# One core, four layers of attention and experts: learned-key attention by whole chunks, and divisions, stores and roots joined to their neighbours

## The reference, cut to what matters

```
def _layernorm(x, axis=-1, eps=1e-05):
    m = jnp.mean(x, axis=axis, keepdims=True)
    v = jnp.var(x, axis=axis, keepdims=True)
    return (x - m) / jnp.sqrt(v + eps)

def pattention(x, K, V):                 # K, V: learned, 128 keys (512 for the last one)
    a = softmax(scale * einsum('btc,nc->btn', x, K), axis=-1)
    return einsum('btn,nc->btc', a, V)

# layer 0 attention: softmax attention over q, k, v, then
# out = a_dot * (1 - w) + a_mem * w, where a_mem = (sigma_q @ memory) / (sigma_q @ memory_norm)

# layer 1 attention
        h = layer_norm(x)
        k = pattention(h, kK, kV)
        q = pattention(h, qK, qV)
        v = pattention(h, vK, vV)
        ...
        o = causal_sdpa(to_heads(q), to_heads(k), to_heads(v))
        o = o.transpose(0, 2, 1, 3).reshape(B, T, C)
        o = pattention(o, pK, pV)
        x = o + x_in
        x_inter = x
        x = pattention(layer_norm(x), fK, fV)
        return x + x_inter
```

## Time and profile before

| | us |
|---|---|
| median of 3 runs | 3603.91 (3601.78 to 3606.88) |
| profiled execution | 3613.86 |
| its span | 3612.1 |
| granted PE clock, mean over the span | 0.926 of full |
| busy: PE, DVE, ACT, POOL | 3240.8, 2450.0, 1820.7, 1191.2 |

### The profile page before, as it was taken

How to read it: one execution, slowest core, us unless ns; L and a number is a source line. 1 busy time by engine, 2 the same in 40 slices (tenths; PEclk the granted TensorE clock), 3 DMA queues, 4 the chain that set the end, 5 groups by cost and what they waited for, 6 DMA issues and landing times. The chain is left out here.

```text
span 3612.1 us, 39566 instructions
## 1 busy us (share of the span) xinstructions
PE 3240.8 (90%) x12845; PEld 1536.3 (43%) x12845; DVE 2450.0 (68%) x4164; ACT 1820.7 (50%) x2881; POOL 1191.2 (33%) x1010
## 2 busy tenths in 40 slices
PE   8899998999997699979998789898898789889999
PEld 5422224444444354535544233333333354764443
DVE  4788874443338577746544899999999955656544
ACT  5366672444446355534333777777777633312221
POOL 4211110000002222210000799999999910210000
PEclk7699998999998799989899899999999979889999
DMA  4222201000002533110000443443443410000000
GB/s 129 66 69 65 61 31 33 1 0 1 1 19 81 132 88 91 60 39 1 1 1 25 153 153 147 148 157 144 155 152 147 147 45 3 1 1 1 0 1 24
DMA packets 113335, 232.14 MB, mean 64 GB/s; under 512 B 27701, under 2 KB 82378, under 8 KB 95754
## 3 DMA queue, kind: packets, MB, share of 16 engines
q1 hardware_dynamic: 109034, 228.02, 19.0%
q0 software_dynamic: 4096, 1.59, 0.2%
HBM read 191.46 MB, written 34.87 MB: 63 GB/s over the span
## 5 line engine op out<-in xcount | busy, mean ns | idle before, releaser
L1199 DVE TENSOR_REDUCE a_top<-a_sc 128x1 f32<-128x512 f32 (+3 forms) x1024 | 547.2, 584 | 162.3 <-PE a_sc L1075 102.5
L2406 POOL TENSOR_TENSOR a_g<-a_g,a_spread 128x1024 f32<-128x1024 f32 x255 | 597.7, 2363 | 41.4 <-DVE a_g L2336 40.8
L2336 DVE TENSOR_TENSOR_SCAN a_g<-a_decay,a_drive 128x512 f32<-128x512 f32 x510 | 587.1, 1201 | 16.3 <-ACT a_drive L2225 12.9
L1156 ACT ACTIVATE a_prob<-a_st 128x1024 f32<-128x1024 f32 (+2 forms) x512 | 422.5, 862 | 280.7 <-PE a_st L1092 182.9
L705 DVE TENSOR_TENSOR f_s<-f_a,f_spread 128x512 f32<-128x512 f32 x392 | 269.4, 687 | 381.8 <-PE f_y L547 170.6
L2084 PE MATMUL a_y<-a_g,ident 128*128 128x512 f32 x1024 | 481.0, 610 | 31.3 <-POOL a_g L2406 31.3
L538 PE MATMUL f_hid<-h,f_w 128*128 128x512 f32 x784 | 404.2, 597 | 0.0
L547 PE MATMUL f_y<-f_s,f_w 128*128 128x512 f32 x784 | 401.6, 594 | 2.6 <-DVE f_s L705 2.6
L2209 ACT ACTIVATE a_decay<-a_delta,a_capped_a 128x512 f32<-128x512 f32 x512 | 331.8, 710 | 12.4 <-DVE a_g L2336 9.7
L1072 PE MATMUL a_sc<-a_k,a_q 96*128 96x512 bf16 (+3 forms) x1024 | 311.4, 357 | 20.9 <-POOL a_mask_k L996 11.2
L2084 PEld LDWEIGHTS a_y<-a_g,ident 128*128 128x128 f32 x1024 | 198.4, 197 | 306.7 <-issue 246.1
(11 more groups left out here) (396 smaller groups left out, 4903.0 us busy)
## 6 DMA issues: line engine op xcount, KB each, us to landing
a_spread<-a_bc_rows SPq DMA_DIRECT2D x128, 1024.0 KB, 4.6
a_q<-a_q_rows SPq DMA_DIRECT2D x192, 96.0 KB
a_pv_rows<-a_pv_sb SPq DMA_DIRECT2D x48, 256.0 KB, 2.0
a_k<-a_k_rows SPq DMA_DIRECT2D x288, 32.0 KB
a_k<-a_k_rows SPq DMA_DIRECT2D x288, 16.0 KB
a_num<-a_pv_rows SPq DMA_DIRECT2D x16, 256.0 KB, 3.6
a_pv_rows<-a1q_vf SPq DMA_DIRECT2D x16, 256.0 KB, 2.1
a_q_rows<-p_qp SPq DMA_DIRECT2D x24, 128.0 KB
```

Of the source, the lines that this page charges most:

```text
L1156: nc.scalar.activation(prob[w % 2][:, j, 0:width(kp)], st[:, j % 2, 0:width(kp)], ACT.Exp, scale=a.scale).then_inc(s.exp_done, 1)
L1199: nc.vector.tensor_reduce(top[:, t, n:n + 1], sc[:, slot(4 * n + t) % 3, 0:w], AX.X, ALU.max).then_inc(s.maxed, 1)
L2336: nc.vector.tensor_tensor_scan(to, decay[:, n % 4, k, way], drive[:, k, way], 0.0, ALU.mult, ALU.add).then_inc(scanned, 1)
L2406: nc.gpsimd.tensor_tensor(g[:, n % 8, :, :], g[:, n % 8, :, :], spread[:, pair % 4, 2 + n % 2:3 + n % 2, :].to_broadcast([P, H2, L]), ALU. ...
```

## The change

It has seven parts.

1. **Roots**: the Newton step is one reciprocal and three instructions that each do two operations.
2. **Output**: f3 stores each chunk of the output itself, after its last addition.
3. **Division**: `combine` uses buffers that `attend` has left free (`a.q`, `a.k`). Near the end of `attend`, SP loads the denominators of the first seven chunks and the numerators of chunks 0 to 3, POOL builds the selection matrices, and DVE takes the reciprocal. The denominators of the last chunk are loaded in `combine`, spread over 64 rows, and inverted as a 128x128 tile. The wait for the last store moves from `attend` into SP's list in `combine`.
4. **Learned keys**: a1p has a function of its own, `pattention_one`, which goes by chunks.
5. **layer0_project**: `copy_num` and `widen` stand ahead of the three squares.
6. **a1q**: the parts of k are stored ahead of those of q.
7. **Mamba**: one small Silu is put into its layer norm's block.

```diff
@@ layer_norm (the same in layer_norm_twice and mixture)
-            nc.vector.tensor_scalar(v[:, :], var[:, :], EPS, None, ALU.add)
             chain(nc.vector.reciprocal(rstd[:, :], std[:, :]))
-            chain(nc.vector.tensor_tensor(v[:, :], v[:, :], rstd[:, :], ALU.mult))
-            chain(nc.vector.tensor_tensor(v[:, :], v[:, :], rstd[:, :], ALU.mult))
-            chain(nc.vector.tensor_scalar(v[:, :], v[:, :], -0.5, 1.5, ALU.mult, ALU.add))
-            chain(nc.vector.tensor_tensor(rstd[:, :], rstd[:, :], v[:, :], ALU.mult))
+            chain(nc.vector.scalar_tensor_tensor(v[:, :], var[:, :], EPS, rstd[:, :], ALU.add, ALU.mult))
+            chain(nc.vector.scalar_tensor_tensor(v[:, :], v[:, :], -0.5, rstd[:, :], ALU.mult, ALU.mult))
+            chain(nc.vector.scalar_tensor_tensor(rstd[:, :], v[:, :], 1.5, rstd[:, :], ALU.add, ALU.mult))
@@ mixture, sync engine
+            if out is not None:
+                for c in range(NB):
+                    sp.wait_ge(f.added, c + 1)
+                    sp.dma_start(out[:, chunk(c)], S.x[:, chunk(c)]).then_inc(S.stored, 16)
+                sp.wait_ge(S.stored, 16 * NB)
@@ attend, sync engine
             for b in range(1, NB):
                 body(b, True, True, b % 2)
+            sp.wait_ge(s.st_done, (nB + NB - 1) * 32)
+            for k in range(2):
+                sp.wait_ge(s.pv_stored[k], 16 * 2 * (nB + NB - 1))
+            sp.dma_start(m.den[0:EARLY, :], m.rows[0:EARLY, DH, :]).then_inc(m.den_loaded, 16)
+            for b in range(4):
+                sp.dma_start(m.num[:, b, :], m.rows[H * b:H * b + H, 0:DH, :]).then_inc(m.num_loaded[b], 16)
             body(NB, False, True, 0)
-            for k in range(2):
-                sp.wait_ge(s.pv_stored[k], 16 * 2 * (nB + NB))
+            a.pv_landed = [(s.pv_stored[k], 16 * 2 * (nB + NB)) for k in range(2)]
@@ attend, POOL and DVE, at the end of their lists
+            pool.wait_ge(s.st_done, (nB + NB - 1) * 32)
+            build_picks(nc, pool, m)
...
+            dve.wait_ge(m.den_loaded, 16 * m.call + 16)
+            nc.vector.reciprocal(m.den[0:EARLY, :], m.den[0:EARLY, :]).then_inc(m.inverse, 1)
@@ layer0_project, scalar engine
+                if c >= 1:
+                    copy_num(c - 1)
+                    widen(c - 1)
                 for n in jobs_of(c):
...
                     nc.scalar.activation(sq[n % 3][:, 0:jobs[n].shape[1]], jobs[n], ACT.Square).then_inc(squared, 1)
-                if c >= 1:
-                    copy_num(c - 1)
-                    widen(c - 1)
@@ combine, sync engine, PE, DVE (EARLY = 112)
+            for landed, value in a.pv_landed:
+                sp.wait_ge(landed, value)
+            sp.wait_ge(m.picked, 5 * m.call + 5)
+            for q in range(4):
+                sp.dma_start(m.den_last[32 * q:32 * q + H, :], m.rows[EARLY:EARLY + H, DH, q * P:(q + 1) * P]
+                             ).then_inc(m.last_loaded, 16)
+            for b in range(4, NB):
+                sp.wait_ge(m.multiplied, NB * m.call + b - 3)
+                sp.dma_start(m.num[:, b % 4, :], m.rows[H * b:H * b + H, 0:DH, :]).then_inc(m.num_loaded[b % 4], 16)
...
+                if b < NB - 1:
+                    last = nc.tensor.matmul(inv[:, b % 4, :], m.pick[0:EARLY, b, :], m.den[0:EARLY, :],
+                                            start=True, stop=True)
+                else:
+                    pe.wait_ge(m.last_inverse, m.call + 1)
+                    for q in range(4):
+                        last = nc.tensor.matmul(inv[:, b % 4, q * P:(q + 1) * P], m.pick_last[:, q, :], m.den_last,
+                                                start=True, stop=True)
...
+                if b == 5:
+                    dve.wait_ge(m.last_loaded, 64 * m.call + 64)
+                    nc.vector.reciprocal(m.den_last, m.den_last).then_inc(m.last_inverse, 1)
@@ pattention, a1q's stores
+                    sp.wait_ge(pj.k_parts, pc + c + 3)
+                    store_parts(sp, a.k_rows, c, kp[k], pj.stored[k])
                     sp.wait_ge(pj.q_parts, pc + c + 3)
                     store_parts(sp, a.q_rows, c, qp[k], pj.stored[k])
-                    sp.wait_ge(pj.k_parts, pc + c + 3)
-                    store_parts(sp, a.k_rows, c, kp[k], pj.stored[k])
@@ new: pattention_one, the three lists
+            scores(0)
+            scores(1)
+            for c in range(NB):
+                turn(c)
+                if c + 2 < NB:
+                    scores(c + 2)
+                if c >= 1:
+                    product(c - 1)
+            product(NB - 1)
...
+            exps(0)
+            for c in range(NB):
+                if c + 1 < NB:
+                    exps(c + 1)
+                take(c)
...
+            negate(0)
+            for c in range(NB):
+                if c + 1 < NB:
+                    negate(c + 1)
+                norm(c)
+                if c >= 1:
+                    dve.wait_ge(summed, c)
+                    merge(dve, c - 1, y[:, (c - 1) % 2, :])
+            dve.wait_ge(summed, NB)
+            merge(dve, NB - 1, y[:, (NB - 1) % 2, :])
@@ Mamba, scalar engine's part beside its layer norm
+                nc.scalar.activation(warm[:, :], S.eps[:, 0:1], ACT.Silu)
```

More of the change, by code:

```diff
@@ L451, in last_of, with _ @@
             return k // G * U + groups[k % G][-1]
-        if pending:
-            @block.sync
-            def _(sp):
-                if clears:
-                    sp.wait_ge(S.cleared, n_cleared)
-                for to, what, sem in pending:
-                    sp.dma_start(to, what).then_inc(sem, 16)
+        @block.sync
+        def _(sp):
+            if clears and pending:
+                sp.wait_ge(S.cleared, n_cleared)
+            for to, what, sem in pending:
+                sp.dma_start(to, what).then_inc(sem, 16)
+            if out is not None:
[3 more added lines that the diff above has]
+                sp.wait_ge(S.stored, 16 * NB)
         @block.tensor
@@ L819, in attention_semaphores @@
     S.at = s
+    S.division = (sem("dv_den_loaded"), sem("dv_inverse"), sem("dv_picked"), sem("dv_last_loaded"), sem("dv_last_inverse"),
+                  [sem(f"dv_num_loaded{k}") for k in range(4)], sem("dv_spread"), sem("dv_multiplied"))
     S.setup_primes += [(s.maxed, 3), (s.exp_done, 2), (s.pv_done, 2), (s.evacuated, 2)]
@@ L872, in attend @@
     s, KVH, HK = S.at, a.KVH, H // a.KVH
+    m = a.merge = combine_buffers(S, a)
     call = s.calls
@@ L1558, in _ @@
+        @block.tensor
+        def _(pe):
+            pe.wait_ge(m.picked, 5 * m.call + 5)
+            pe.wait_ge(m.inverse, m.inverses + 1)
             for b in range(NB):
                 if b >= 4:
-                    sp.wait_ge(multiplied, b - 3)
-                sp.dma_start(num[:, b % 4, :], rows[H * b:H * b + H, 0:DH, :]).then_inc(num_loaded[b % 4], 16)
-        @block.gpsimd
-        def _(pool):
-            nc.gpsimd.memset(pick[:, :, :], 0.0).then_inc(picked, 1)
-            pool.wait_ge(picked, 1)
-            view = pick[:, :, :].rearrange("k b (h d) -> k (b h) d", d=DH)
-            nc.gpsimd.affine_select(out=view, in_=view, compare_op=ALU.not_equal, fill=1.0, base=0,
-                                    pattern=[[-1, P], [0, DH]], channel_multiplier=1).then_inc(picked, 1)
@@ L1572, in _ @@
-        @block.tensor
-        def _(pe):
-            pe.wait_ge(picked, 2)
-            pe.wait_ge(inverse, 1)
-            for b in range(NB):
-                if b >= 4:
-                    pe.wait_ge(multiplied, b - 3)
-                nc.tensor.matmul(inv[:, b % 4, :], pick[:, b, :], den[:, :], start=True, stop=True).then_inc(spread, 1)
+                    pe.wait_ge(m.multiplied, NB * m.call + b - 3)
+                if b < NB - 1:
[6 more added lines that the diff above has]
+                                                start=True, stop=True)
@@ L1896, in layer1_attention @@
         attend(nc, S, a)
+        combine(nc, S, a, g)
         held.close()
-        combine(nc, S, a, g)
         def merge_inner(dve, c, y):
@@ L1903, in layer1_attention @@
         s.merged_base = 0
-        pattention(nc, S, "a1p", g, pkeys[:, :], [pvalues[:, :]], [1], merge=merge_inner)
+        pattention_one(nc, S, "a1p", g, pkeys[:, :], pvalues[:, :], merge_inner)
         layer_norm(nc, S, g, S.h)
@@ L2963, in build @@
         if "f3" in stages:
-            mixture(nc, S, fs["f3"])
-        with nc.Block() as block:
-            @block.sync
-            def _(sp):
-                sp.dma_start(out, S.x[:, :]).then_inc(S.stored, 16)
-                sp.wait_ge(S.stored, 16)
+            mixture(nc, S, fs["f3"], out)
         last.close()
```

149 lines of the change are left out of this document (115 added, 34 removed).

## The result

The changed kernel takes 3568.78 us (median of 4 runs, 3568.32 to 3569.17) against 3605.39 for the kernel before on the same chip. The ratio is 0.9895, 95% interval 0.9877 to 0.9913: faster by 1.05%, some 38 us. The forecast was 3574.2 (29.7 less), the range 3560 to 3590. Direction and range held; the gain was 7 to 8 us larger.

The account below looks back on a forecast made before the run. PE is busy for 90% of the span, mostly in untouched work; the touched stages are chains of waits. Terms −7.6−7.5+2.0−3.0−1.3+0−6.7−1.2−4.4 = −29.7, taken off the median 3603.91, give 3574.2 us, range 3560 to 3590.

Parts of the forecast that it names:

- Division: End of attend and combine: PE starts sooner, most of the reciprocal done earlier; −7.6 us in layer 0, −7.5 in layer 1.
- Early loads: Near the end of attend: 1.25 MB of loads delay POOL's maxima, 1.0 us per attention, +2.0 in all.
- Rival C: Early loads delay the maxima by 4.65 us in both attentions, giving 3581.5; chance 0.12.
- Roots, Silu, output: Shorter roots −3.0 us, Silu table loaded beside Mamba's layer norm −1.3, last output store only 256 KB −4.4.
- a1p: Learned keys by chunks: no change from 46.2 us, bounds −8.0 and +8.2, with DVE and PE taking turns.
- the middle, 46.2: a1p's assumed length: between 44 us at clock 0.79 (42% of time at half) and 48 at 0.65 (70%).
- The sum for the full clock: a1p's chunk steps added with PE at full clock: 4.8 us per middle chunk, 38.2 in all; at half 54.4.
- rival B: a1p runs at half clock throughout, giving 3582.4 us in total; chance 0.22.
- layer0_project: With the copies ahead, PE no longer waits for the widened inverse: −6.7 us, bounds −3 and −11.
- Rival D: The project stage gives back its gain, ACT's copies now holding up the squares and PE's sums: 3580.9; chance 0.12.
- k before q: In a1q SP stores k's ready parts instead of waiting for q's: −1.2 us, bounds −0.4 and −1.9.
- Rival E: Nothing overlaps in a1p: 84 us instead of 46.2, total 3612.0, slower than before; chance 0.015.

Follow-up runs that it names:

- experiment 6: Kernel before with only the shorter roots, output stored by chunk and early Silu table: 3598.09 us, ratio 0.9991 (0.9981 to 1.0002).
- experiment 3: Changed kernel with the old stage of learned keys, by tiles, put back in a1p: 3564.39 us, ratio to before 0.9894.
- experiment 4: Kernel before with only the two copies ahead of the three squares in layer0_project: 3599.10 us, ratio 0.9985 (0.9974 to 0.9997).
- experiments 4 to 6: Besides experiment 4 and experiment 6, the one between: kernel before with only the joined division of attend and combine, 3582.14 us, ratio 0.9943.

## Why the prediction was right, point by point

- **Division.** Mechanism right, size low: −9.0 and −8.3 (or −8.2) against −7.6 and −7.5. In layer 0 the term taken too large was the 13.64 from PE's first pass to the end, which I carried over whole and put 0.95 on top for the reciprocal, 14.6. It held 0.95 of a PE at half clock after a long wait; measured are 13.2 with the reciprocal in it. In layer 1 the numerators of chunks 4 to 7 came late, as said: DVE idles 1.78 us before chunk 4, and 0.26 before the last two. Chunk 4 was multiplied 6.85 us behind the last store's issue where I had 7.2, and from there to the end it was 3.64 where I had 4.08.
- **Early loads.** +2.0 was too much: under 1 us of new wait, nothing in the stage's length. Rival C fell: the longest single wait in 500 to 560 was 1.0.
- **Roots, Silu, output.** Each is in its place with the size given: 0.32 per root, 1.28, 4.6. (Nine times 0.33 and once 0.23 are 3.2, not the 3.0 that I wrote.) Only together they are not seen in the time of experiment 6.
- **a1p.** The forecast of 0 was off by +4.6 to +5.0 in the change's own traces, and by 0 to +5 over the four traces with this stage. The step that failed is the choice of the clock, "the middle, 46.2". At a like clock, 0.77, the old and the new stage take 44.8 and 45.2 (experiment 3), so the 0 is right there; the change's own two traces had 0.66 and 0.67 where before had 0.79. The sum for the full clock, 38.2, was measured as 38.3. That for half clock, 54.4, no run shows, and the rule between them is 1 to 2 us short: for 0.66 it gives 48, and 50.1 was measured, for 0.77 44.3 and 45.2. So the clock explains about 2 of the 4 to 5 us by my own rule; the other 2 or so stay open, perhaps because the chain costs more at a low clock than I summed. Of rival B, half clock throughout and 54.4, the measured 50 is as far as of the forecast. Its reading of the Trainium skill ("TensorE: Matmul & The Clock Gate", Part 1), by which half rate is the default and PE with these pauses stays there, agrees with the trace only in part: 0.66 lies between the two levels, and 1.00 came once PE had idle work. The sign that DVE's waits and PE's would be about alike failed too: 27.1 us against 17.9. In the time the part can't be told from nothing (experiment 3).
- **layer0_project.** The wait of PE for the widened inverse is gone but for 0.2 us in the first trace and one wait of 1.5 in the second. The gain of 6.7 was mis-sized: 11.6 and 13.1 in the changed kernel, beyond the bound of 11, and the sign "a project stage of 97 to 103 us" failed (90.5 in the window that answers to the earlier trace rows). At a like clock the order gives 7.7 to 8.2 (experiment 4), near what I had. The rest goes with the clock, 0.73 and 0.76 instead of 0.64, and that the new order raises it is likely, not shown: the old order had 0.64 to 0.73 in four traces and the new one 0.69 to 0.81 in ten. Rival D fell.
- **k before q.** −1.7 to −2.4 against −1.2.
- **The sum.** Against the forecast: division −2.2, early loads −2, the projection −5, a1p +4.5, k −0.8, output −0.2, in all −5.7. With −29.7 that is −35.4, of a measured 36.6 by the medians and 38 by the ratio. Rival E, no overlap at all, was not near: 50 and not 84. The projection and a1p were wrong in opposite directions, in both cases by the clock that I took for the stage: that these two errors cancel is luck, and the forecast is nearer than its terms. The parts measured alone (experiments 4 to 6) add up to −29, not −38; their intervals are wide enough for the difference, and no run shows where it lies.

## What to carry to other kernels

Fewer and larger instructions gain nothing by themselves where two engines take turns: with 40 of DVE's instructions for 136, a1p was as long as before at the same mean clock. What halved it was the order: the scores ahead of the transposes (32.4 alone), the merge one chunk later (30.2 alone), and both with the maximum one chunk further ahead (23.6). Before merging instructions, write down for one step which engine waits for which, and put every consumer far enough behind its producer that the double buffer is in use. In this stage PE's pauses cost twice, once as themselves and once as clock: with idle work in them it went from 50 to 38 us. So pauses spread through a stage are worth looking for first. And where identical code differs by 5 us from trace to trace, compare stages at a like granted clock before giving a difference to an edit.

## What the runs showed of the hardware

- **Pauses and the granted clock.** PE was busy for 31.5 of 50.1 us in a1p and granted 0.66; with scores first it was busy for 19.7 of 32.4 and granted 1.00. Before its transposes PE waited 17.9 us in eight waits, none over 2.6, in the first and 10.4 in seven in the second. 32 passes of idle work turned the first into 38.3 us at 1.00. So short pauses alone went with a mean between the two levels, and one order had the full clock throughout in its trace. I had expected the clock to lie between two values that other stages showed.
- **The same program, other clocks.** f0's stretch, the same code but for a root that is 0.3 us shorter, took 515.2 to 520.7 in fourteen traces, and the two traces of one kernel were 520.7 and 515.3.
- **Small transfers beside bulk.** With 1.25 MB being loaded on SP's queue, the longest landing of POOL's 12 KB transfers in layer 0's last passes was 3.5 us, against 2.1 without.
